# Finer steps in the attention part of a gated cross-attention and expert block: layer norms by pairs of blocks, a bias product in two parts, another order of TensorE's work

## The chip, the core and the metric

One core of a Trainium2 chip runs the whole program in one launch. The metric is the device time of one execution in microseconds (us). Five engines work side by side, each through its own queue in order: TensorE (PE in the rows; its loads of weights are PEld), VectorE (DVE), ScalarE (ACT), GpSimd (POOL) and SyncE (SP). They meet at semaphores only: an instruction waits until a counter has reached a value, and everything behind it in its queue waits too.

## What is computed

Inputs are `x` and a context, both 8 blocks x 128 rows x 128 columns, float32. Cut to what matters:

```
x = x + tanh(g_xattn) * attention(q = layernorm(x), k = v = context)    # Wq, Wk, Wv, Wo, biases; softmax per block
x = x + tanh(g_ffn)   * ffn(layernorm(x))
ffn(y)    = shared(y) + routed(y)
shared(y) = (silu(y @ w1) * (y @ w2)) @ w3       # hidden width 512
routed(y) = sum over 16 experts of gate * swiglu(y), hidden width 128;
            the gates are the sigmoid scores of the 2 best experts of each row
layernorm = (x - mean) / sqrt(var + 1e-5)        # no learned weights
```

## The kernel before

A row of a block lies in a partition; a block of 128x128 is the unit. The 8 blocks are two halves of 4 (`HALF`), and a half is two pairs of blocks. There is no scheduler: each engine's queue is written out by hand, in the order in which it stands in the code, with the waits between engines written by hand too. So a step that stands ahead of another in a queue is done first, even if it must wait and the other could go.

**The attention part, one half after the other.** DVE takes the statistics of the blocks (`block_stats`, `moments`: L549, L555, L557), POOL raises variance plus epsilon to the power -0.5 for a half at a time (`inverse_deviation`, L376, tile `rstd`), and the blocks are normalised into `xn`. PE turns them (transposes against `ident`), ACT copies them to `xnT`. Wq and Wk are fused into `qk_w`, Wv and Wo into `vo_w`. PE then makes g = `qk_w` x `xnT` for pair p (`query_key`, L831), ACT copies it to `gT` (`copy_g`), PE makes the scores (`attention_scores`, L836), DVE the row maxima, ACT the exponentials (`probs`), PE turns them (`turn_probs`), a copy gives `probsT`, and PE multiplies them with `vo` (`attend`, L848). `vo` is context x `vo_w` (`value_output`, L827) plus `vo_bias`. That bias row is the sum of two products in one bank (`fused_bias`): bv against Wo turned (L876), and a column of ones against the row bo (L877). DVE adds the attention to `x` (`add_attention`, L616) and gets `x2`.

**The second layer norm.** The statistics of `x2` follow (`second_stats`); POOL gives `rstd` again; of each half DVE normalises the first two blocks (L568) and ACT the last two (L453, with `shift` = -mean x rstd from DVE). PE turns the pairs (`turn_x2n_pair`, L858), DVE and ACT copy one pair each to `x2nT`.

**The products.** Work goes by chunks k. `share_up(k)` (L927, L928) multiplies 512 columns of `x2nT` by two blocks of weights, ACT takes the silu (L484), DVE multiplies to `hid` (L648), `share_down(k)` (L944) multiplies that by the third block. Chunks 0 to 3 are the shared part of the first half, 4 to 7 of the second half, 8 to 12 two often-used experts; then small tiles of the other experts follow. The router's logits need `x2nT` of both halves and stand on PE between `share_down(2)` and `share_down(3)`. The second half's attention, from its second transposes of `probs` on, is worked in between the first chunks: `share_up(0)`, `turn_probs(2)`, `share_up(1)`, `turn_probs(3)`, `attend(2)`, `attend(3)`, `share_down(0)`, `share_up(2)`, `share_down(1)`, `share_up(3)`, then the transposes of the second half's `x2n`. `keep_warm` (L807) issues products whose result nobody reads.

## Time and profile before

| | us |
|---|---|
| median of 3 runs (lowest to highest) | 74.22 (73.93 to 74.92) |
| the profiled execution | 73.88 |
| its span, first to last instruction | 72.2 |
| PE busy in the span | 60.9 (84%) |
| DVE, ACT, POOL busy | 38.8, 26.0, 11.7 |

The profiled execution's own time is 1.68 us more than its span: what lies around the instructions. Times in rows are from the span's start. Each matrix product in float32 shows as two matmul records with one load of weights each. Matmuls are pipelined: a record lasts longer than the distance to the next one, so a series is costed by the distance between starts.

### The profile page before, as it was taken

What the parts mean: (1) busy time and instruction counts of PE and PEld (TensorE: products, weight loads), DVE (VectorE), ACT (ScalarE), POOL (GpSimd) and SP (SyncE); (2) the same over time, 40 slices, a digit from 0 to 9 for tenths busy, and PEclk for the clock granted to TensorE, in tenths of its full rate; (3) what the DMA queues carried; (4) which work ended last, traced back from release to release, by engine and by line L of the source; (5) the groups of instructions that cost most, each with busy time, mean ns of one, the idle gap of its engine ahead of it and who ended that gap; (6) DMA issues with size and microseconds to landing.
All of it is one profiled execution on the core that took longest, in us unless ns stands there. A gap on an engine that the chain in (4) does not pass through costs nothing.

```text
span 72.2 us, 1153 instructions
## 1 busy us (share of the span) xinstructions
PE 60.9 (84%) x341; PEld 42.9 (60%) x342; DVE 38.8 (54%) x159; ACT 26.0 (36%) x71; POOL 11.7 (16%) x26
## 2 busy tenths in 40 slices
PE   1997998596979995999999999999999999996200
PEld 0335877574744564576984577475676998884100
DVE  2074824688332259833569795864730398765300
ACT  0334858043738930044411323031156823332000
POOL 4005099804100000140000000000005260000000
PEclk9999999999999999999999999999999999999985
DMA  0898470000000000000000000610698300000560
GB/s 0 229 321 203 119 313 24 0 0 0 0 0 9 0 0 5 0 0 0 0 0 0 0 0 5 189 37 0 198 283 250 145 5 0 0 0 5 148 157 13
DMA packets 5084, 4.80 MB, mean 66 GB/s; under 512 B 336, under 2 KB 4816, under 8 KB 5072
## 3 DMA queue, kind: packets, MB, share of 16 engines
q1 hardware_dynamic: 3984, 3.93, 17.8%
q10 hardware_dynamic: 1088, 0.74, 3.6%
q14 instruction: 9, 0.07, 0.3%
q8 instruction: 3, 0.05, 0.3%
HBM read 4.15 MB, written 0.52 MB: 65 GB/s over the span
## 4 chain that ended last, share of the span: by engine, by line
PE 72%; DVE 9%; DMA 4%; issue 3%; ACT 3%; POOL 1%; DVEq 0%; POOLq 0%
PE bank L944 15%; PE bank L927 15%; PE bank L928 14%; DMA x_sb<-in_x_dram 4%; PE bank L831 3%; PE bank L827 3%; PE bank L1013 3%; PE bank L822 2%; PE bank L965 2%; PE bank L836 2%; PE bank L848 2%; PE bank L1005 2%; PE bank L1004 2%; DVE hid L648 2%; PE bank L807 1%
## 5 line engine op out<-in xcount | busy, mean ns | idle before, releaser
L648 DVE TENSOR_TENSOR hid<-silu_t,bank 128x512 f32<-128x512 f32 (+1 forms) x13 | 8.4, 645 | 9.8 <-ACT silu_t L484 8.5
L484 ACT ACTIVATE silu_t<-bank 128x512 f32<-128x512 f32 (+1 forms) x13 | 7.3, 563 | 15.3 <-PE bank L928 15.3
L944 PEld LDWEIGHTS bank<-shared_sb,hid 128*128 128x128 f32 x64 | 8.1, 191 | 3.7 <-issue 1.9
L944 PE MATMUL bank<-shared_sb,hid 128*128 128x128 f32 x64 | 8.7, 280 | 0.9 <-DVE hid L648 0.9
L927 PE MATMUL bank<-x2nT,shared_sb 128*128 128x512 f32 x16 | 8.3, 603 | 0.6 <-ACT x2nT L475 0.6
L928 PE MATMUL bank<-x2nT,shared_sb 128*128 128x512 f32 x16 | 8.2, 592 | 0.0
L376 POOL TENSOR_TENSOR rstd<-var_eps,neg_half 128x4 f32<-128x4 f32 x4 | 4.1, 1018 | 21.3 <-DVE var_eps L557 21.3
L807 PE MATMUL bank<-warm_rows 128*128 128x512 bf16 x14 | 5.3, 530 | 1.6 <-DVE warm_rows L578 1.5
L410 POOL TENSOR_TENSOR acc<-acc,gated 128x512 f32<-128x512 f32 x2 | 2.5, 1270 | 24.9 <-ACT gated L494 24.9
L928 PEld LDWEIGHTS bank<-x2nT,shared_sb 128*128 128x128 f32 x16 | 3.0, 190 | 3.8 <-issue 3.8
L944 PEld LDWEIGHTS bank<-dense_w,hid 128*128 128x128 f32 x32 | 4.1, 191 | 1.9 <-issue 1.0
L944 PE MATMUL bank<-dense_w,hid 128*128 128x128 f32 x32 | 4.5, 278 | 0.7 <-DVE hid L648 0.7
L927 PE MATMUL bank<-x2nT,dense_w 128*128 128x512 f32 (+1 forms) x10 | 4.4, 518 | 0.0
L928 PE MATMUL bank<-x2nT,dense_w 128*128 128x512 f32 (+1 forms) x10 | 4.3, 507 | 0.0
L807 PEld LDWEIGHTS bank<-warm_rows 128*128 128x128 bf16 x15 | 1.8, 128 | 4.0 <-issue 2.2
L848 PE MATMUL bank<-vo,probsT 128*128 128x128 f32 x16 | 2.7, 292 | 1.2 <-DVE probsT L602 1.1
L453 ACT ACTIVATE x2n<-x,shift,rstd 128x128 f32<-128x128 f32 x4 | 1.7, 484 | 5.4 <-DVE shift L563 5.4
L1013 PE MATMUL bank<-tile_w,tile_hid 128*128 128x128 f32 x16 | 3.2, 294 | 0.2 <-DVE tile_hid L672 0.2
L501 ACT ACTIVATE tile_silu<-bank 128x128 f32<-128x128 f32 x8 | 2.1, 282 | 3.4 <-PE bank L1005 3.4
L927 PEld LDWEIGHTS bank<-x2nT,shared_sb 128*128 128x128 f32 x16 | 2.5, 193 | 1.2 <-issue 1.2
L848 PEld LDWEIGHTS bank<-vo,probsT 128*128 128x128 f32 x16 | 2.1, 190 | 1.8 <-DVE vo L592 1.3
L684 DVE SCALAR_TENSOR_TENSOR acc<-bank,tile_gates,acc 128x128 f32 x8 | 2.8, 348 | 0.7 <-issue 0.3
(135 smaller groups left out, 103.1 us busy)
## 6 DMA issues: line engine op xcount, KB each, us to landing
tile_w<-in_routed_w_dram SPq DMA_DIRECT2D x8, 192.0 KB, 3.6
shared_sb<-in_shared_w_dram SPq DMA_DIRECT2D x1, 768.0 KB, 4.5
dense_w<-in_routed_w_dram SPq DMA_DIRECT2D x2, 192.0 KB, 2.5
params<-in_attn_params_dram ACTq DMA_DIRECT2D x1, 265.0 KB, 4.1
ctx_sb<-in_ctx_dram SPq DMA_DIRECT2D x1, 256.0 KB, 4.0
x_sb<-in_x_dram SPq DMA_DIRECT2D x1, 256.0 KB, 5.6
ctx_sb<-in_ctx_dram ACTq DMA_DIRECT2D x1, 256.0 KB, 5.8
out_dram<-acc SPq DMA_DIRECT2D x1, 256.0 KB, 2.6
```

Of the source, the lines that this page charges most:

```text
L376: pool.tensor_tensor(rstd[:, n, halves(h)], var_eps[:, n, halves(h)], neg_half[:, :], ALU.pow)\
L410: pool.tensor_tensor(acc[:, h * 512:(h + 1) * 512], acc[:, h * 512:(h + 1) * 512], gated[:, i % 2, :], ALU.add)\
L484: nc.scalar.activation(silu_t[:, k % 2, columns(k)], bank[up_bank(k)][:, columns(k)], ACT.Silu).then_inc(silu_ready, 1)
L648: nc.vector.tensor_tensor(hid[:, k % HID_RING, columns(k)], silu_t[:, k % 2, columns(k)], bank[up_bank(k) + 1][:, columns(k)], ALU.mult)\
L684: nc.vector.scalar_tensor_tensor(acc[:, bass.ds(to, D)], tile_down_bank(t), tile_gates[:, t:t + 1], acc[:, bass.ds(to, D)], ALU.mult, ALU. ...
L807: nc.tensor.matmul(bank[spare][:, :], warm_rows[:, 0:P], warm_rows[:, :], start=True, stop=True)
L827: last = nc.tensor.matmul(bank[7 - h][:, b * P:(b + 1) * P], ctxT[:, HALF * h + b, :], vo_w[:, :], start=True, stop=True)
L848: last = nc.tensor.matmul(bank[S_BANK[p]][:, (b % 2) * P:(b % 2 + 1) * P], probsT[:, b, :], vo[:, b, :], start=True, stop=True)
L927: nc.tensor.matmul(bank[up_bank(k)][:, columns(k)], w1, xt, start=True, stop=True)
L928: nc.tensor.matmul(bank[up_bank(k) + 1][:, columns(k)], w2, xt, start=True, stop=True).then_inc(up_done, 1)
L944: last = nc.tensor.matmul(down_bank(k, b)[:, b * P:(b + 1) * P], hid[:, k % HID_RING, b * P:(b + 1) * P], down_weights(k), start=first and ...
L1013: nc.tensor.matmul(tile_down_bank(t), tile_hid[:, t % 3, :], tile_w[:, t % W_RING, 2 * P:3 * P], start=True, stop=True)\
```

## The change

Six things are edited, all in the attention part and the second layer norm up to the first products.

1. The first half's first layer norm goes by pairs: `x_loaded` has one semaphore for each of the three loads of x, and `moments`, `inverse_deviation` and the normalising work on PARTS: blocks 0 and 1, blocks 2 and 3, blocks 4 to 7. POOL computes three powers instead of two, here and in the second layer norm.
2. The bias product is in two parts: the product with bv stays behind `query_key(0)`, the product with ones moves between the scores of pair 0 and pair 1.
3. `turn_probs(1)` moves ahead of `attend(0)`; the turning of `xn`'s second half ahead of `value_output(1)`.
4. The first half's second layer norm goes by pairs too. DVE normalises blocks 0, 1 and 2, ACT only block 3. `values(1)` moves behind the row maxima of pairs 2 and 3. Pair 0 is turned into bank 3 instead of bank 6, between `query_key(3)` and the scores of pairs 2 and 3. Both calls of `keep_warm` there are gone.
5. Chunk 0's products go by pairs of blocks, 256 columns each.
6. On DVE `share(0)` stands ahead of `add_attention(2)`, and `second_stats(2)` ahead of `add_attention(3)`.

```diff
+        PARTS = (slice(0, 2), slice(2, 4), slice(4, 8))
...
-            def inverse_deviation(n, h):
-                pool.wait_ge(var_ready, 2 * n + h + 1)
-                pool.tensor_tensor(rstd[:, n, halves(h)], var_eps[:, n, halves(h)], neg_half[:, :], ALU.pow)\
+            def inverse_deviation(n, m):
+                pool.wait_ge(var_ready, 3 * n + m + 1)
+                part = PARTS[m]
+                pool.tensor_tensor(rstd[:, n, part], var_eps[:, n, part], neg_half[:, 0:part.stop - part.start], ALU.pow)\
                     .then_inc(rstd_ready, 1)
...
-            normalise(0)
+            normalise((3,), 1)
             act.wait_ge(x2n_pair_turned, 2)
...
-            dve.wait_ge(x_loaded[0], 16 * 2)
-            block_stats(0, x_sb, range(HALF))
-            moments(0, 0)
-            dve.wait_ge(rstd_ready, 1)
-            normalise(0, x_sb, xn, range(HALF), xn_by_dve)
-            dve.wait_ge(x_loaded[1], 16)
+            for m in range(2):
+                dve.wait_ge(x_loaded[m], 16)
+                block_stats(0, x_sb, range(2 * m, 2 * m + 2))
+                moments(0, m)
+            for m in range(2):
+                dve.wait_ge(rstd_ready, m + 1)
+                normalise(0, x_sb, xn, range(2 * m, 2 * m + 2), xn_by_dve)
+            dve.wait_ge(x_loaded[2], 16)
...
-            add_attention(0)
-            second_stats(0)
-            add_attention(1)
-            second_stats(1)
-            moments(1, 0)
-            values(1)
-            shifts(0)
+            for p in range(2):
+                add_attention(p)
+                second_stats(p)
+                moments(1, p)
+            dve.wait_ge(rstd_ready, 4)
             normalise(1, x2, x2n, (0, 1), x2n_by_dve)
             dve.wait_ge(x2n_pair_turned, 1)
-            nc.vector.tensor_copy(x2nT[:, 0:256], bank[6][:, 0:256]).then_inc(x2nT_ready[0], 1)
+            nc.vector.tensor_copy(x2nT[:, 0:256], bank[3][:, 0:256]).then_inc(x2nT_ready[0], 1)
+            shifts(1)
+            normalise(1, x2, x2n, (2,), x2n_by_dve)
             row_maxima(2)
             row_maxima(3)
+            values(1)
...
+            def first_share_up():
+                w1, w2 = up_weights(0)
+                for p in range(2):
+                    pe.wait_ge(x2nT_ready[p], 1)
+                    c = slice(256 * p, 256 * p + 256)
+                    nc.tensor.matmul(bank[up_bank(0)][:, c], w1, x2nT[:, c], start=True, stop=True)
+                    last = nc.tensor.matmul(bank[up_bank(0) + 1][:, c], w2, x2nT[:, c], start=True, stop=True)
+                last.then_inc(up_done, 1)
...
             pe.wait_ge(x2_ready, HALF)
-            share_up(0)
+            first_share_up()
             turn_probs(2)
+            pe.wait_ge(vo_ready[1], 1)
             share_up(1)
```

PE's queue around the bias product, before. Bank 6 takes the bias product, banks 0 and 1 take g, banks 2 and 3 the scores:

```order
L831 MATMUL bank0<-xnT,qk_w 128x256 [waits xnT_ready0,fused_ready]
L876 MATMUL bank6<-woT,params 128x128 [waits vo_w_ready,rows_loaded,consts_ready]
L877 MATMUL bank6<-rows,ones_row 128x128
L831 MATMUL bank1<-xnT,qk_w 128x256 [waits xnT_ready1]
L836 MATMUL bank2<-ctxT,gT 128x128 [waits g_ready0,ctxT_ready0]
L836 MATMUL bank2<-ctxT,gT 128x128
L836 MATMUL bank3<-ctxT,gT 128x128 [waits g_ready1]
L836 MATMUL bank3<-ctxT,gT 128x128
```

And of the changed kernel, where the lines are numbered otherwise (L838 is `query_key`, L843 the scores, L890 and L897 the bias product's parts):

```order
L838 MATMUL bank0<-xnT,qk_w 128x256 [waits xnT_ready0,fused_ready]
L890 MATMUL bank6<-woT,params 128x128 [waits vo_w_ready]
L838 MATMUL bank1<-xnT,qk_w 128x256 [waits xnT_ready1]
L843 MATMUL bank2<-ctxT,gT 128x128 [waits g_ready0,ctxT_ready0]
L843 MATMUL bank2<-ctxT,gT 128x128
L897 MATMUL bank6<-rows,ones_row 128x128 [waits rows_loaded,consts_ready]
L843 MATMUL bank3<-ctxT,gT 128x128 [waits g_ready1]
L843 MATMUL bank3<-ctxT,gT 128x128
```

The product with ones has moved from ahead of `query_key(1)` to between the two pairs of scores.

PE's queue from `query_key(2)` to the first product, before (L858 turns `x2n`, L836 are scores, L807 the products nobody reads):

```order
L831 MATMUL bank5<-xnT,qk_w 128x256 [waits xnT_ready2]
L831 MATMUL bank4<-xnT,qk_w 128x256
L807 MATMUL bank7<-warm_rows 128x512 x2
L836 MATMUL bank5<-ctxT,gT 128x128 [waits g_ready2]
L836 MATMUL bank5<-ctxT,gT 128x128
L836 MATMUL bank4<-ctxT,gT 128x128 [waits g_ready3]
L836 MATMUL bank4<-ctxT,gT 128x128
L807 MATMUL bank7<-warm_rows 128x512 x3
L858 MATMUL bank6<-ident,x2n 128x128 [waits x2n_by_dve,vo_ready1]
L858 MATMUL bank6<-ident,x2n 128x128
L858 MATMUL bank7<-ident,x2n 128x128 [waits x2n_by_act]
L858 MATMUL bank7<-ident,x2n 128x128
L927 MATMUL bank2<-x2nT,shared_sb 128x512 [waits x2nT_ready0,x2_ready,shared_loaded]
```

And of the changed kernel (L867 turns `x2n`, L940 and L941 are the first chunk's products by pairs):

```order
L838 MATMUL bank5<-xnT,qk_w 128x256 [waits xnT_ready2]
L838 MATMUL bank4<-xnT,qk_w 128x256
L867 MATMUL bank3<-ident,x2n 128x128 [waits x2_ready,x2n_by_dve]
L867 MATMUL bank3<-ident,x2n 128x128
L843 MATMUL bank5<-ctxT,gT 128x128 [waits g_ready2]
L843 MATMUL bank5<-ctxT,gT 128x128
L843 MATMUL bank4<-ctxT,gT 128x128 [waits g_ready3]
L843 MATMUL bank4<-ctxT,gT 128x128
L867 MATMUL bank7<-ident,x2n 128x128 [waits x2n_by_act,x2n_by_dve]
L867 MATMUL bank7<-ident,x2n 128x128
L940 MATMUL bank2<-x2nT,shared_sb 128x256 [waits x2nT_ready0,x2_ready,shared_loaded]
L941 MATMUL bank3<-x2nT,shared_sb 128x256
```

The turning of pair 0 now stands ahead of the scores, with a wait for DVE, and the five products on `warm_rows` are gone.

DVE's queue from the second half's scale to the second product, before (L648 is `hid`, L616 adds the attention):

```order
L609 TENSOR_SCALAR att_scale<-inv_sum,tanh_g 128x4 [waits tanh_ready,inv_ready]
L616 SCALAR_TENSOR_TENSOR x2<-bank5,att_scale,x_sb 128x128 [waits pv_done,att_scale_ready]
L616 SCALAR_TENSOR_TENSOR x2<-bank5,att_scale,x_sb 128x128
L648 TENSOR_TENSOR hid<-silu_t,bank3 128x512 [waits silu_ready]
L616 SCALAR_TENSOR_TENSOR x2<-bank4,att_scale,x_sb 128x128 [waits pv_done,att_scale_ready]
L616 SCALAR_TENSOR_TENSOR x2<-bank4,att_scale,x_sb 128x128
L549 BN_STATS stats<-x2 128x6 [waits x2_ready]
L549 BN_STATS stats<-x2 128x6
L549 BN_STATS stats<-x2 128x6 [waits x2_ready]
L549 BN_STATS stats<-x2 128x6
L648 TENSOR_TENSOR hid<-silu_t,bank7 128x512 [waits silu_ready]
L555 BN_AGGR mean_var<-stats 128x2 [waits stats_ready] x4
```

And of the changed kernel (L655 is `hid`, L622 adds the attention):

```order
L615 TENSOR_SCALAR att_scale<-inv_sum,tanh_g 128x4 [waits tanh_ready,inv_ready]
L655 TENSOR_TENSOR hid<-silu_t,bank3 128x512 [waits silu_ready]
L622 SCALAR_TENSOR_TENSOR x2<-bank5,att_scale,x_sb 128x128 [waits pv_done,att_scale_ready]
L622 SCALAR_TENSOR_TENSOR x2<-bank5,att_scale,x_sb 128x128
L553 BN_STATS stats<-x2 128x6 [waits x2_ready]
L553 BN_STATS stats<-x2 128x6
L622 SCALAR_TENSOR_TENSOR x2<-bank4,att_scale,x_sb 128x128 [waits pv_done,att_scale_ready]
L622 SCALAR_TENSOR_TENSOR x2<-bank4,att_scale,x_sb 128x128
L553 BN_STATS stats<-x2 128x6 [waits x2_ready]
L553 BN_STATS stats<-x2 128x6
L655 TENSOR_TENSOR hid<-silu_t,bank7 128x512 [waits silu_ready]
L559 BN_AGGR mean_var<-stats 128x2 [waits stats_ready] x4
```

`hid` of chunk 0 has moved ahead of both additions, and both additions with their statistics now stand between it and `hid` of chunk 1.

## Rows read from the trace of the kernel before

**Rows 1.** The page: the clock granted to TensorE, in 40 slices of the span (tenths)

```profile
PEclk9999999999999999999999999999999999999985
```

**Rows 2.** Busy time of each engine in three stretches

```profile
core 0: us, PE busy (x) PEld busy (x) DVE busy (x) ACT busy (x) POOL busy (x), PEclk, DMA share, GB/s
12.20:15.60 3.40, 2.31 (x17) 1.83 (x16) 2.46 (x9) 1.30 (x4) 2.01 (x10) 1.00 0.00 0
15.60:19.00 3.40, 2.67 (x17) 2.10 (x19) 2.78 (x13) 1.15 (x3) 1.04 (x1) 1.00 0.00 0
28.00:59.00 31.00, 30.98 (x174) 21.71 (x175) 18.61 (x82) 9.78 (x24) 3.55 (x3) 1.00 0.21 64
```

**Rows 3.** The chain that ended last, around the bias product (start us, us, what)

```profile
8.91 0.41 PE bank L877 x2
...
10.52 0.71 PE bank L836 x4
```

**Rows 4.** Instructions in order of time, from 3.8 to 10 us

```profile
3.81 0.87 DVE L549 BATCH_NORM_STATS2 stats<-x_sb 128x6 f32<-128x128 f32 x4 [2.34 <-DMA x_sb<-in_x_dram]
...
5.00 0.17 DVE L557 TENSOR_SCALAR var_eps<-mean_var 128x4 f32<-128x4 f32 x1
5.32 1.02 POOL L376 TENSOR_TENSOR rstd<-var_eps,neg_half 128x4 f32<-128x4 f32 x1 [3.60 <-DVE var_eps L557]
...
7.74 0.38 PE L869 MATMUL bank<-ident,xn 128*128 128x128 f32 x2
...
8.42 0.38 ACT L432 COPY xnT<-bank 128x256 f32<-128x256 f32 x1
...
9.26 0.70 PE L831 MATMUL bank<-xnT,qk_w 128*128 128x256 f32 x2
...
9.79 1.44 PE L836 MATMUL bank<-ctxT,gT 128*128 128x128 f32 x8
...
10.02 3.12 POOL L384 TENSOR_SCALAR xn<-x_sb,mean_var,rstd 128x128 f32<-128x128 f32 x4
```

**Rows 5.** The same from 14 to 22 us

```profile
14.21 0.61 DVE L616 SCALAR_TENSOR_TENSOR x<-bank,att_scale,x_sb 128x128 f32<-128x128 f32 x2 [0.59 <-PE bank L848]
...
14.86 0.49 DVE L549 BATCH_NORM_STATS2 stats<-x 128x6 f32<-128x128 f32 x2
...
15.59 0.61 DVE L616 SCALAR_TENSOR_TENSOR x<-bank,att_scale,x_sb 128x128 f32<-128x128 f32 x2 [0.25 <-PE bank L848]
...
17.29 1.04 POOL L376 TENSOR_TENSOR rstd<-var_eps,neg_half 128x4 f32<-128x4 f32 x1 [3.00 <-DVE var_eps L557]
...
18.44 0.60 DVE L568 TENSOR_SCALAR x2n<-x,mean_var,rstd 128x128 f32<-128x128 f32 x2
...
19.24 0.86 ACT L453 ACTIVATE x2n<-x,shift,rstd 128x128 f32<-128x128 f32 x2
...
20.63 0.60 PE L858 MATMUL bank<-ident,x2n 128*128 128x128 f32 x4
...
21.27 0.37 ACT L475 COPY x2nT<-bank 128x256 f32<-128x256 f32 x1 [1.17 <-PE bank L858]
...
21.79 1.10 PE L927 MATMUL bank<-x2nT,shared_sb 128*128 128x512 f32 x2 [0.55 <-ACT x2nT L475]
```

**Rows 6.** The chain again: transposes of `probs`, `share_down(1)`, `share_down(2)`

```profile
25.68 0.23 PE bank L842 x2
...
30.90 0.89 PE bank L944 x8
...
33.95 1.01 PE bank L944 x8
```

**Rows 7.** Instructions in order of time, from 27 to 34 us

```profile
27.29 0.68 DVE L648 TENSOR_TENSOR hid<-silu_t,bank 128x512 f32<-128x512 f32 x1
...
29.18 0.67 DVE L648 TENSOR_TENSOR hid<-silu_t,bank 128x512 f32<-128x512 f32 x1
...
33.06 0.69 DVE L648 TENSOR_TENSOR hid<-silu_t,bank 128x512 f32<-128x512 f32 x1 [0.91 <-ACT silu_t L484]
```

More of the change, by code:

```diff
@@ L175, in flamingo_block @@
         ctx_loaded = [sem(f"ctx_loaded{i}") for i in range(2)]
-        x_loaded = [sem(f"x_loaded{i}") for i in range(2)]
+        x_loaded = [sem(f"x_loaded{i}") for i in range(3)]
         shared_loaded = sem("shared_loaded")
@@ L220, in flamingo_block @@
         x2n_turned = sem("x2n_turned")
-        x2nT_ready = [sem(f"x2nT_ready{i}") for i in range(2)]
+        x2nT_ready = [sem(f"x2nT_ready{i}") for i in range(3)]
         x2n_pair_turned = sem("x2n_pair_turned")
@@ L399, in _ @@
                                base=0, pattern=[[1, P]], channel_multiplier=-1).then_inc(route_consts_ready, 1)
-            inverse_deviation(1, 0)
-            inverse_deviation(1, 1)
+            for m in range(3):
+                inverse_deviation(1, m)
             for k in range(FIRST_DENSE, FIRST_DENSE + BY_POOL):
@@ L890, in _ @@
             attention_scores(0)
+            pe.wait_ge(consts_ready, 2)
+            pe.wait_ge(rows_loaded, 16)
+            nc.tensor.matmul(bank[6][:, P:2 * P], ones_row[:, :], bo_row, start=False, stop=True).then_inc(fused_done, 1)
             attention_scores(1)
```

84 lines of the change are left out of this document (39 added, 45 removed).

## The prediction

> **What bounds the kernel now.** Read the busy time by stretches first. From 28 to 59 us PE is busy 30.98 of 31.00 us, and in the two stretches between 12.2 and 19 us only 2.31 and 2.67 of 3.40 [rows 2]. So the program is two things: up to 28 us a ladder of short steps that hand over between engines, and then a block of TensorE work with no holes. None of the change's edits takes useful work out of that block. What it can gain is an earlier start of the block, and what it can lose is a hole in it. The question is therefore when `hid` of chunk 0 ends (27.29 + 0.68 = 27.97 [rows 7]), since `share_down(0)` and everything behind it follows, and whether the DVE work that the change pushes behind it comes late for something. Then read the chain of waits and the order of time through the ladder, and ask at each rung: does this instruction start when its data are there, or only when its own queue gets to it?
>
> **Part a: up to the scores of pair 1.** In the chain the product with ones takes 0.41 us [rows 3], the one with bv ahead of it has two records of 0.11, and both stand between `query_key(0)` and `query_key(1)`. `query_key(1)` starts at 9.26, though its `xnT` was copied by 8.42 + 0.38 = 8.80 [rows 4]. So 0.46 us there is waiting in PE's own queue, not for data.
> The layer norm by pairs, step by step. Four blocks of statistics take 0.87 us and the epsilon step starts 1.19 us after the first of them (3.81 to 5.00). With two blocks fewer I take 0.70, so it starts at 4.51 and ends at 4.68; POOL starts about 0.10 later, at 4.78. The power of 4 columns takes 1.02 [rows 4]. The trace has none of 2 columns. Its cost lies between 0.51 (all of it goes by columns) and 1.02 (none of it does). The only row is that of 4 columns, so I take 1.02, the end that this row states. Then pair 0's power ends at 5.80, where the whole half's ended at 6.34: pair 0 is 0.54 early. Pair 1's power queues behind it on POOL, ends at 6.82, and pair 1 is normalised by 7.46, as before (about 7.48). So the pairs help pair 0 alone, and pair 1 gains only what PE's queue gave away: its turning starts at about 7.53 instead of 7.74 [rows 4]. The ACT copies in front are done earlier too, thanks to pair 0, so that `xnT` of pair 1 is ready at 7.53 + 0.48 + 0.41 = 8.42, and `query_key(1)` starts at 8.52, 0.74 early.
> From there to the scores of pair 1 it was 10.52 - 9.26 = 1.26 [rows 3, 4], so they could start at 9.78. But the product with ones now stands in front of them: the scores of pair 0 start 0.53 behind `query_key(1)`, at 9.05; eight records of scores are 0.11 apart, so four take 0.43, and with 0.10 of transition and 0.41 the product with ones is through at 9.99; I take 9.95. The gain is 10.52 - 9.95 = 0.57. With the cheap power it would be `query_key(1)` at 8.31 and 9.78 at the scores, 0.74. The low end is 0.2, if the product with ones holds up the scores longer than its 0.41.
>
> **Part b: to the attention's addition.** From the scores of pair 1 to `x2` of pair 0 it was 14.21 - 10.52 = 3.69 [rows 3, 5], through `value_output(0)`, the addition of the bias on DVE, the copy of `probsT` and `attend(0)`. All of it stands in the same order. `turn_probs(1)` now waits for the last exponential ahead of `attend(0)`, but PE sat idle there for the copy, and two transposes are 0.23 us [rows 6]. Cost 0. It brings `attend(1)` forward, which is the cover that part c needs: `x2` of pair 1 came 1.38 us behind pair 0 [rows 5], and will again, though four small steps are put between them. The addition starts at 13.64.
>
> **Part c: from the first addition to the first product.** Before, 21.79 - 14.21 = 7.58 us [rows 5]. Count what the data alone need in the new order, from the start of the first addition: addition and wait 0.65 (14.21 to 14.86); statistics of two blocks, aggregates, epsilon start 0.67; next instruction 0.08: 1.40. The same again for pair 1: 2.80. DVE normalises two blocks, 0.60: 3.40. Turning and handing over 0.47: 3.87. DVE copies, 0.43: 4.30. The shift and its handing over, in part under the copy: 4.42. ACT normalises one block, 0.48 (half of 0.86, a little more): 4.90. PE turns pair 1, 0.05 + 0.25 later the first product starts: 5.20 to 5.25. POOL's power for pair 1 starts at 2.97 and ends by 4.05 even at 1.04 us, hidden under the turning and the copy. The gain is 7.58 - 5.25 = 2.33 us.
> Where did the time lie before? `x2n` was whole at 19.24 + 0.86 = 20.10, but PE turned it at 20.63, behind the scores and the products on `warm_rows`; and the power started at 17.29 because it waited for all four blocks [rows 5]. ACT's part started 0.80 behind DVE's because ACT was copying g.
> Can PE keep up? `attend(0)` starts 0.80 ahead of the addition, at 12.84. Behind it, at 0.11 a record: the second half of its own four records and a hand-over 0.43, four transposes 0.43, `attend(1)` 0.43, four transposes 0.43, eight records of values 0.86 and `query_key(2)` and (3) 0.86 give 16.4 with a wait or two. Pair 0's `x2n` is there at 13.64 + 3.45 = 17.1. So PE waits 0.7 us in `turn_x2n_pair(0)`, with the scores of pairs 2 and 3 queued behind it; DVE's row maxima for these wait in turn, but stand behind `x2n` of block 2 anyway. POOL's second half of `xn` is done at 13.14 [rows 4], ahead of its turning at about 14.2. The second half's `values(1)`, 0.69 us of DVE, is out of this stretch, which is part of the 2.33. Bounds from the neighbours: 1.8 (every hand-over 0.05 longer, ten of them) to 2.6.
>
> **Part d: from the first product to `hid` of chunk 0.** Before, 27.97 - 21.79 = 6.18. Chunk 0 by 256 columns issues the same columns; I allow 0.04. The chain turns the `probs` of pair 3 from 25.68 [rows 6], and behind their copy and the scale stood one addition, then `hid`. An addition of two blocks is 0.61 long [rows 5], 0.54 of it before the next instruction starts. This addition now comes behind `hid`. ACT's silu of chunk 0 waits for the second half's exponentials and a load of tables. They start 0.9 us behind the turning of pair 1 and are through about 1.3 us before `hid`, as I count it. Gain 0.50.
>
> **Part e: what is late behind `hid` of chunk 0.** Before, `hid` of chunk 1 started 29.18 - 27.97 = 1.21 us behind it. Now two additions and two pairs of statistics lie between: 0.65 + 0.43 + 0.65 + 0.41, less 0.09 of overlap, 2.05. `share_down(1)` was due 30.90 - 27.97 = 2.93 behind [rows 6], and `hid` of chunk 1 ends at 2.05 + 0.68 = 2.73: covered, by 0.2. But the second half's statistics, power and normalising follow it, and ACT normalises blocks 6 and 7 ahead of the silu of chunk 2. From the start of `hid` of chunk 1 to the end of that of chunk 2 it was 33.75 - 29.18 = 4.57 [rows 7], so now it ends at 6.62, and `share_down(2)`, which stood at 33.95 - 27.97 = 5.98 [rows 6], waits until 6.65. A hole of 0.67 us in the block, and the logits and the router move with it. Bounds: 0.3 to 0.9.
>
> **Sum.** 0.57 + 2.33 + 0.50 - 0.67 = 2.73 us. 73.88 - 2.73 = 71.15 against the profiled execution, which was 0.34 below the median of 74.22; with half of that, **71.3**. The ends of the parts, not all at once, give 70.4 to 72.1.
>
> **Rivals.** (1) TensorE's clock. The granted clock is full until the last slices, after PE has gone quiet [rows 1]. The change takes out the five products on `warm_rows` and puts in a wait of 0.7 us at about 16.5, then one of 0.4. Fell the clock there from 2.4 to 1.2 GHz until `share_down(0)`, the 6.1 us of records up to it (transposes 0.88, scores 0.86, products 3.5, `attend` 0.86) would take twice as long, less 1.1 of waits that this fills: 5.0 more, 76.1 us. It turns into a loss against before once more than 2.7 us of records fall at the lower level. Against it: from 12.2 to 15.6 PE was busy 2.31 of 3.40, and the clock stayed at 1.00 [rows 2]. The new stretch packs the same work closer.
> The Trainium skill speaks for this rival: TensorE: Matmul & The Clock Gate, Part 4 (PE-mode transpose), says that transposes don't count as activity for the full clock as products do. The stretch of 12.2 to 15.6 holds six transposes among 17 records and kept 1.00, which bears out at most that such a mixture is enough here; no row shows one without `warm_rows` ahead of the products.
> (2) PE comes late to `turn_x2n_pair(0)`. The margin is 0.7 us. Were the turned `xn` and its copy, now ahead of `value_output(1)`, or the wait for `ctxT` 2 us late, 1.3 would be lost: 72.6.
> (3) The pairs and the split product give nothing, since the second power queues on POOL and the ones product stands in front of the scores: part a is 0, 71.9. That is the form in which the change would not do what it says.
> (4) The hole grows: `hid` of chunk 1 misses its 0.2 of cover too and the router's steps on DVE fall behind PE, 1.5 instead of 0.67: 72.1, with part c at its low end 72.7.
>
> **How the numbers follow.** Forecast 0.70; (1) 0.08, of which 0.05 in full; (2) 0.06; (3) 0.09; (4) 0.07. A measurement of this kernel can tell some 2% from no change, so faster means below 72.74 and slower above 75.70. Faster holds the forecast, (3) and most of (2) and (4), 0.84; slower the full form of (1), 0.05; the rest is 0.11. For 8 in 10 the range goes from 70.4 to 72.9.
>
> **What would show it.** `query_key(1)` starts near 8.5 and the scores of pair 1 near 9.95, right behind the product with ones. Two powers of about 1 us stand back to back on POOL near 4.8 and 5.8. The first product starts near 18.9, 5.2 us behind the first addition. PE idles ahead of the turning of pair 0. `hid` of chunk 0 ends near 24.5. One new wait stands in the block, of 0.6 to 0.7 us at `share_down(2)`; behind it PE is full as before. I am wrong if the granted clock dips between 16 and 25 us, if PE's idle time at the first turning is gone (then PE, not DVE, sets part c), or if the block has other holes.

## The result

The changed kernel takes 71.48 us (70.98 to 71.82, 4 runs) against 74.08 us before (4 runs): ratio 0.9665, 95% interval 0.9622 to 0.9708. Measured a second time beside other kernels it gave 0.966 (0.959 to 0.9731). It is faster, by 2.6 us; 71.3 was forecast. Executions more than 1.5% above a kernel's fastest are left out of the ratios here and below, but are in the medians.

The profiled execution took 71.56 us, its span is 69.7. The page of the changed kernel, busy time and the two rows over 40 slices:

```profile
PE 60.0 (86%) x341; PEld 42.9 (62%) x341; DVE 39.7 (57%) x162; ACT 25.5 (37%) x70; POOL 12.5 (18%) x28
...
PE   1999998796899989979999999999999999995100
...
PEclk9999999999999999999999999999999999999985
```

Beside [rows 1] the granted clock reads the same: full until the last slices. The stretches, laid where the same work now is:

```profile
core 0: us, PE busy (x) PEld busy (x) DVE busy (x) ACT busy (x) POOL busy (x), PEclk, DMA share, GB/s
12.20:15.60 3.40, 2.99 (x24) 2.75 (x25) 2.75 (x13) 1.47 (x3) 1.81 (x10) 1.00 0.00 0
15.60:19.00 3.40, 2.60 (x18) 1.95 (x16) 2.80 (x14) 1.47 (x4) 1.33 (x2) 1.00 0.00 0
...
24.70:56.50 31.80, 31.21 (x174) 21.49 (x175) 19.33 (x85) 9.78 (x24) 3.54 (x3) 1.00 0.20 63
```

From 12.2 to 15.6 PE is busy 2.99 of 3.40, where it was 2.31 [rows 2]. And the block behind `share_down(0)`, which had no hole, has one. PE is busy 31.21 of 31.80; 0.11 of the rest lies ahead of `share_down(0)`, which starts at 24.81, and 0.48 is the wait shown below.

The changed kernel's instructions in order of time, from 4 to 12 us. Its lines are L878 for the turning of `xn`, L838 for `query_key`, L843 for the scores, L821 to L825 for the fusing of the weights, L890 and L897 for the two bias products:

```profile
4.43 0.17 DVE L561 TENSOR_SCALAR var_eps<-mean_var 128x2 f32<-128x2 f32 x1
...
4.75 1.43 POOL L380 TENSOR_TENSOR rstd<-var_eps,neg_half 128x2 f32<-128x2 f32 x2 [3.04 <-DVE var_eps L561]
...
5.50 1.32 DVE L572 TENSOR_SCALAR xn<-x_sb,mean_var,rstd 128x128 f32<-128x128 f32 x4
5.77 0.35 PE L821 MATMUL bank<-ident,params 128*128 128x128 f32 x1
...
6.48 0.49 PE L825 MATMUL bank<-woT,params 128*128 128x128 f32 x2
...
6.81 0.38 PE L878 MATMUL bank<-ident,xn 128*128 128x128 f32 x2
...
7.74 0.67 PE L838 MATMUL bank<-xnT,qk_w 128*128 128x256 f32 x2
...
8.57 0.70 PE L838 MATMUL bank<-xnT,qk_w 128*128 128x256 f32 x2
...
9.13 0.68 PE L843 MATMUL bank<-ctxT,gT 128*128 128x128 f32 x4
...
9.75 0.48 PE L897 MATMUL bank<-rows,ones_row 1*128 1x128 f32 x2
...
10.16 0.52 PEld L843 LDWEIGHTS bank<-ctxT,gT 128*128 128x128 f32 x4
```

`xn` of pair 0 is done at about 6.1, but PE turns it at 6.81: it is still at the weights. Before, PE had been through with those by 6.19 + 0.49 and waited for `xn` until 7.03. `query_key(1)` starts at 8.57 (9.26 in [rows 4]), and the scores of pair 1 at 10.16, right behind the product with ones. POOL's two powers take 1.43 together.

The second layer norm and the first products of the changed kernel (L622 adds the attention, L867 turns `x2n`, L940 is the first product):

```profile
16.77 0.59 DVE L572 TENSOR_SCALAR x2n<-x,mean_var,rstd 128x128 f32<-128x128 f32 x2
16.94 0.72 POOL L380 TENSOR_TENSOR rstd<-var_eps,neg_half 128x2 f32<-128x2 f32 x1 [0.73 <-DVE var_eps L561]
...
17.42 0.44 PE L867 MATMUL bank<-ident,x2n 128*128 128x128 f32 x2 [0.55 <-DVE x2n L572]
...
17.70 1.06 PE L843 MATMUL bank<-ctxT,gT 128*128 128x128 f32 x8
...
18.42 0.49 ACT L457 ACTIVATE x2n<-x,shift,rstd 128x128 f32<-128x128 f32 x1 [1.04 <-DVE shift L567]
...
19.06 0.41 PE L867 MATMUL bank<-ident,x2n 128*128 128x128 f32 x2 [0.31 <-ACT x2n L457]
...
19.30 0.60 PE L940 MATMUL bank<-x2nT,shared_sb 128*128 128x256 f32 x2
...
19.51 0.37 ACT L479 COPY x2nT<-bank 128x256 f32<-128x256 f32 x1 [0.59 <-PE bank L867]
...
24.07 0.68 DVE L655 TENSOR_TENSOR hid<-silu_t,bank 128x512 f32<-128x512 f32 x1
...
26.74 0.67 DVE L655 TENSOR_TENSOR hid<-silu_t,bank 128x512 f32<-128x512 f32 x1
...
29.22 0.88 ACT L457 ACTIVATE x2n<-x,shift,rstd 128x128 f32<-128x128 f32 x2 [5.46 <-DVE shift L567]
...
30.01 0.57 ACT L488 ACTIVATE silu_t<-bank 128x512 f32<-128x512 f32 x1
...
30.25 0.63 PE L829 MATMUL bank<-ident,x2n 128*128 128x128 f32 x4
...
30.61 0.69 DVE L655 TENSOR_TENSOR hid<-silu_t,bank 128x512 f32<-128x512 f32 x1 [0.91 <-ACT silu_t L488]
...
31.36 1.16 PE L958 MATMUL bank<-shared_sb,hid 128*128 128x128 f32 x8 [0.48 <-DVE hid L655]
```

In [rows 5] the turning started at 20.63 and the first product at 21.79. Now pair 0 is turned at 17.42 as soon as DVE has it (PE waited 0.55 us for it), and the first product starts at 19.30. At `share_down(2)` stands the new wait: 0.48 us for `hid` of chunk 2, whose silu started at 30.01 only, behind ACT's 0.88 us of normalising. The same place before:

```profile
33.34 0.60 PE L822 MATMUL bank<-ident,x2n 128*128 128x128 f32 x4
...
33.80 1.16 PE L944 MATMUL bank<-shared_sb,hid 128*128 128x128 f32 x8
```

From the transposes to `share_down(2)` it was 0.46 us from start to start, now it is 1.11: the wait is worth 0.65.

Both executions cut into stages, by starts of instructions read from the two traces (us). The spans are printed to 0.1 only, so the last row and the sum are good to some 0.05:

| stage | before | changed | gain |
|---|---|---|---|
| start to `query_key(0)` | 8.02 | 7.74 | 0.28 |
| to the first addition of attention | 6.19 | 6.11 | 0.08 |
| to the first product | 7.58 | 5.45 | 2.13 |
| to the start of `hid` of chunk 0 | 5.50 | 4.77 | 0.73 |
| to `share_down(2)` | 6.51 | 7.29 | -0.78 |
| to the end of the last addition | 34.05 | 34.05 | 0.00 |
| to the end of the span | 4.35 | 4.29 | 0.06 |
| sum | 72.20 | 69.70 | 2.50 |

From `share_down(2)` to the last addition the two kernels take the same 34.05 us. All of the change's effect lies ahead of it.

### The profile page after: what moved, and what is told of

The parts are those of the page before. It is cut to its first block, busy times and chain, and to the rows that moved or that the text cites. A ratio compares the mean times of both kernels' runs of the same rounds, so it can differ in the third digit from the quotient of the medians.

```text
span 69.7 us, 1158 instructions
## 1 busy us (share of the span) xinstructions
PE 60.0 (86%) x341; PEld 42.9 (62%) x341; DVE 39.7 (57%) x162; ACT 25.5 (37%) x70; POOL 12.5 (18%) x28
## 4 chain that ended last, share of the span: by engine, by line
PE 66%; DVE 17%; issue 5%; ACT 3%; POOL 1%; DVEq 0%
PE bank L958 13%; PE bank L931 12%; PE bank L932 11%; PE bank L814 6%; DVE hid L655 4%; DVE x L622 3%; PE bank L1028 3%; DVE stats L553 3%; PE bank L980 2%; PE bank L1019 2%; PE bank L1020 2%; ACT silu_t L488 2%; PE bank L838 2%; PE bank L843 2%; POOL rstd L380 1%
## 5 line engine op out<-in xcount | busy, mean ns | idle before, releaser
L655 DVE TENSOR_TENSOR hid<-silu_t,bank 128x512 f32<-128x512 f32 (+1 forms) x13 | 8.4, 644 | 9.3 <-ACT silu_t L488 8.1
L488 ACT ACTIVATE silu_t<-bank 128x512 f32<-128x512 f32 (+1 forms) x13 | 7.3, 563 | 14.8 <-PE bank L932 14.8
L958 PEld LDWEIGHTS bank<-shared_sb,hid 128*128 128x128 f32 x64 | 8.0, 191 | 3.8 <-DVE hid L655 2.3
L958 PE MATMUL bank<-shared_sb,hid 128*128 128x128 f32 x64 | 8.8, 280 | 0.7 <-DVE hid L655 0.7
L380 POOL TENSOR_TENSOR rstd<-var_eps,neg_half 128x2 f32<-128x2 f32 (+1 forms) x6 | 4.9, 811 | 18.0 <-DVE var_eps L561 18.0
L931 PE MATMUL bank<-x2nT,shared_sb 128*128 128x512 f32 x14 | 7.2, 599 | 0.0
L932 PE MATMUL bank<-x2nT,shared_sb 128*128 128x512 f32 x14 | 7.1, 592 | 0.0
L814 PE MATMUL bank<-warm_rows 128*128 128x512 bf16 x10 | 4.5, 632 | 1.5 <-DVE warm_rows L582 1.5
L958 PEld LDWEIGHTS bank<-dense_w,hid 128*128 128x128 f32 x32 | 4.1, 192 | 1.9 <-issue 1.0
L958 PE MATMUL bank<-dense_w,hid 128*128 128x128 f32 x32 | 4.5, 278 | 0.7 <-DVE hid L655 0.7
L932 PEld LDWEIGHTS bank<-x2nT,shared_sb 128*128 128x128 f32 x14 | 2.7, 190 | 3.3 <-issue 3.3
L457 ACT ACTIVATE x2n<-x,shift,rstd 128x128 f32<-128x128 f32 x3 | 1.4, 487 | 6.5 <-DVE shift L567 6.5
L553 DVE BATCH_NORM_STATS2 stats<-x_sb 128x6 f32<-128x128 f32 x8 | 1.8, 281 | 2.6 <-DMA x_sb<-in_x_dram 2.6
L388 POOL TENSOR_SCALAR xn<-x_sb,mean_var,rstd 128x128 f32<-128x128 f32 x4 | 3.1, 794 | 0.1
L1019 PE MATMUL bank<-x2nT,tile_w 128*128 x16 | 3.1, 275 | 0.0
L1020 PE MATMUL bank<-x2nT,tile_w 128*128 x16 | 3.1, 275 | 0.0
```

Source lines behind the costliest of these rows:

```text
L380: pool.tensor_tensor(rstd[:, n, part], var_eps[:, n, part], neg_half[:, 0:part.stop - part.start], ALU.pow)\
L388: pool.tensor_scalar(xn[:, b, :], x_sb[:, b, :], mean_var[:, 0, b, 0:1], rstd[:, 0, b:b + 1], ALU.subtract, ALU.mult)\
L488: nc.scalar.activation(silu_t[:, k % 2, columns(k)], bank[up_bank(k)][:, columns(k)], ACT.Silu).then_inc(silu_ready, 1)
L553: nc.vector.bn_stats(stats[:, n, k, :], src[:, k, :]).then_inc(stats_ready, 1)
L655: nc.vector.tensor_tensor(hid[:, k % HID_RING, columns(k)], silu_t[:, k % 2, columns(k)], bank[up_bank(k) + 1][:, columns(k)], ALU.mult)\
L814: nc.tensor.matmul(bank[spare][:, :], warm_rows[:, 0:P], warm_rows[:, :], start=True, stop=True)
```

## The experiments

Each kernel is the changed one with one edit, so each is to be read against 71.5; only the last in the table has three edits and is to be read against the early `hid`. The medians of small edits carry some 0.2 to 0.3 us of scatter. In the traces it is the two ends that vary: the opening (below), and the stretch behind the last addition, 4.0 to 4.5 us in twelve of the profiled executions and 5.5 in two. The stages between are sharper: between kernels that don't touch a stage they agree within 0.02 us. So the verdicts rest on the stages, in this table of differences of starts in each kernel's one profiled execution, with the medians beside them.

| kernel | median us | ratio to before | start to `query_key(0)` | to first addition | to first product | to `hid` 0 | to `share_down(2)` |
|---|---|---|---|---|---|---|---|
| before | 74.08 | 1 | 8.02 | 6.19 | 7.58 | 5.50 | 6.51 |
| changed | 71.48 | 0.9665 | 7.74 | 6.11 | 5.45 | 4.77 | 7.29 |
| changed, again | 71.49 | 0.966 | 8.36 | 6.11 | 5.45 | 4.77 | 7.28 |
| early `hid` of chunk 2 | 70.69 | 0.9549 | 7.54 | 6.10 | 5.46 | 4.77 | 6.63 |
| second norm whole | 72.68 | 0.974 | 7.99 | 6.11 | 6.35 | 6.45 (clock fell) | 7.28 |
| 9 opening products | 71.62 | 0.965 | 7.75 | 6.10 | 5.46 | 4.76 | 7.29 |
| `values(1)` back | 72.18 | 0.9728 | 8.30 | 6.11 | 6.07 | 4.76 | 7.29 |
| turning behind scores | 72.03 | 0.9741 | 7.78 | 6.11 | 6.02 | 4.84 | 7.28 |
| edit 6 undone | 71.62 | 0.9704 | 7.70 | 6.10 | 5.46 | 5.42 | 6.51 |
| `warm_rows` back | 71.70 | 0.9684 | 8.20 | 6.11 | 5.61 | 4.76 | 7.29 |
| first norm whole | 71.84 | 0.9724 | 8.30 | 6.10 | 5.45 | 4.77 | 7.29 |
| bias product whole | 71.67 | 0.9669 | 7.93 | 6.19 | 5.46 | 4.76 | 7.29 |
| `turn_probs(1)` back | 71.47 | 0.9658 | 8.21 | 6.10 | 5.46 | 4.77 | 7.28 |
| early `hid`, short opening | 72.73 | - | 7.92 | 6.10 | 5.46 | 4.76 | 6.64 |

**The hole at `share_down(2)`: pull `hid` of chunk 2 forward.**

```diff
             share(1)                                    # ACT
-            normalise((6, 7), 2)
             share(2)
+            normalise((6, 7), 2)
...
             moments(1, 2)                               # DVE
+            share(2)
             shifts(2)
             normalise(1, x2, x2n, (HALF, HALF + 1), x2n_by_dve)
-            share(2)
```

> The changed kernel with chunk 2 pulled forward: DVE does hid of chunk 2 right behind moments(1, 2), while POOL computes the power, and ACT takes the silu of chunk 2 ahead of normalising blocks 6 and 7. If the new wait at share_down(2) comes from ACT's normalising and DVE's norm work standing ahead of chunk 2 (part e), PE's wait there goes, share_down(2) starts at 30.8 to 30.9 instead of 31.36, and the time falls by 0.45 us, to about 71.0. If the hole is only the first of a series (the router or hid of chunk 3 is late as well), the wait moves behind and the time stays within 0.1 of 71.5.

Measured: 70.69 us, ratio 0.9549 (0.9495 to 0.9603). The last stage is 6.63 instead of 7.29. Its instructions in order of time (L488 is the silu, L655 `hid`, L958 `share_down`, L457 ACT's normalising):

```profile
27.52 0.60 ACT L488 ACTIVATE silu_t<-bank 128x512 f32<-128x512 f32 x1 [3.96 <-PE bank L932]
27.53 0.17 DVE L561 TENSOR_SCALAR var_eps<-mean_var 128x4 f32<-128x4 f32 x1
27.78 1.01 POOL L380 TENSOR_TENSOR rstd<-var_eps,neg_half 128x4 f32<-128x4 f32 x1 [10.32 <-DVE var_eps L561]
28.15 0.69 DVE L655 TENSOR_TENSOR hid<-silu_t,bank 128x512 f32<-128x512 f32 x1 [0.45 <-ACT silu_t L488]
...
28.82 0.16 DVE L567 SCALAR_TENSOR_TENSOR shift<-mean_var,rstd 128x4 f32<-128x4 f32 x1
28.90 0.60 DVE L572 TENSOR_SCALAR x2n<-x,mean_var,rstd 128x128 f32<-128x128 f32 x2
29.02 0.88 ACT L457 ACTIVATE x2n<-x,shift,rstd 128x128 f32<-128x128 f32 x2 [0.90 <-DVE shift L567]
...
30.50 1.06 PE L958 MATMUL bank<-shared_sb,hid 128*128 128x128 f32 x8
```

DVE does `hid` of chunk 2 at 28.15, while POOL computes the power from 27.78, and `share_down(2)` shows no wait. So the hole was order in two queues, not a lack of time, and nothing moved in behind it. The gain of 0.66 in the stage is the 0.65 that the wait was worth. This version beats both kernels.

**The second layer norm as a whole again.**

```diff
-            for m in range(3):
-                inverse_deviation(1, m)
...
+            pool.tensor_tensor(rstd[:, 1, halves(0)], var_eps[:, 1, halves(0)], neg_half[:, :], ALU.pow).then_inc(rstd_ready, 1)
...
                 second_stats(p)
-                moments(1, p)
+            for k in range(HALF):
...
+                nc.vector.bn_aggr(mean_var[:, 1, k, :], stats[:, 1, k, :]).then_inc(moments_ready, 1)
```

> The changed kernel with the first half's second layer norm as before: statistics and one power of 4 columns for all four blocks, everything else as changed. If the pairs are worth something because POOL's power of pair 0 hides under pair 1's addition, then x2n of blocks 0 and 1 comes 1.2 us later, PE turns it near 18.7 instead of 17.42, and the first product starts 0.75 us later: 72.2 us. If the gain of part c came from the order of PE's queue and from moving values(1) alone, it stays at 71.5.

Measured: 72.68 us, ratio 0.974 (0.9671 to 0.9809), which of 74.08 is 72.2 us; the ratio rests on three executions of five, and its interval is wide, so the stage decides. The stage to the first product is 6.35, 0.90 more. PE turns pair 0 at 18.56 and had waited 1.44 us for it. Taken away from the whole change, the pairs cost 0.9 of its 2.13. (In this profiled execution the granted clock fell for a while, so its stage to `hid` 0 is long; see the last section.)

**`values(1)` back ahead of the normalising.**

```diff
                 moments(1, p)
+            values(1)
             dve.wait_ge(rstd_ready, 4)
...
             row_maxima(3)
-            values(1)
```

> The changed kernel with values(1) (0.69 us on DVE) put back ahead of normalising x2n. If DVE's queue sets this rung, as part c counts, the turning of pair 0 and the first product come 0.65 us later, 72.1 us. If PE's queue sets it (rival 2), nothing changes.

Measured: 72.18 us, ratio 0.9728 (0.9671 to 0.9784), the stage 0.62 longer, close to the 0.69 of the instruction. DVE's queue sets this rung.

**The turning of pair 0 behind the scores again.**

```diff
             query_key(3)
-            turn_x2n_pair(0)
             attention_scores(2)
             attention_scores(3)
+            turn_x2n_pair(0)
             turn_x2n_pair(1)
```

> The changed kernel with turn_x2n_pair(0) behind the scores of pairs 2 and 3 again, without the products on warm_rows. The scores could start at 17.0 when g of pair 2 is there; pair 0 would be turned at about 17.95 instead of 17.42, and the copies and the shift behind it on DVE follow. By part c the first product comes 0.4 us later: 71.9 us. If the wait in PE's queue ahead of the scores costs as much as it brings, 71.5.

Measured: 72.03 us, ratio 0.9741 (0.9695 to 0.9787), the stage 0.57 longer. PE's wait of 0.55 us ahead of the scores is well spent.

**The products on `warm_rows` back.**

```diff
             query_key(3)
+            keep_warm(2, 7)
             turn_x2n_pair(0)
...
             attention_scores(3)
+            keep_warm(3, 7)
             turn_x2n_pair(1)
```

> The changed kernel with both series of products on warm_rows put back, 2 ahead of the turning of pair 0 and 3 behind the scores. The granted clock is 1.00 in the changed kernel from 12 to 22 us, so nothing is won; the first two lie in PE's wait, the last three (0.65 us) in a wait of 0.3 to 0.5: 0.15 us later, 71.6. If they held the clock in some executions (rival 1), this kernel would be faster than 71.5 or vary less.

Measured: 71.70 us, ratio 0.9684 (0.9624 to 0.9744), the stage 0.16 longer as expected. Of its four executions one took 73.53 with a mean granted clock of 0.955: the products didn't keep that away.

**Edit 6 undone.**

```diff
-            share(0)
             add_attention(2)
-            second_stats(2)
+            share(0)
             add_attention(3)
+            second_stats(2)
             second_stats(3)
```

> The changed kernel with edit 6 undone: add_attention(2) ahead of hid of chunk 0, add_attention(3) ahead of second_stats(2). By parts d and e this gives back 0.50 to 0.55 at hid of chunk 0 and wins back the wait of 0.5 to 0.6 at share_down(2): the time stays within 0.15 of 71.5. If the hole has another cause, the time rises by 0.5.

Measured: 71.62 us, ratio 0.9704 (0.9676 to 0.9733). `hid` of chunk 0 starts 0.65 later, and the last stage is 6.51 as before, without the hole. Over both stages it is 11.93 against 12.06: edit 6 alone bought nothing and cost 0.13. With the early `hid` of chunk 2 beside it, it is 11.40. The early `hid` without edit 6 was not run; with no wait at `share_down(2)` there, it has nothing to take away.

**The opening, one product on `warm_rows` less.**

```diff
-            keep_warm(10, 7)
+            keep_warm(9, 7)
```

> The changed kernel with 9 instead of 10 opening products on warm_rows. In the changed kernel's trace the transpose of Wo starts at 5.77, behind the last of them, and xn of pair 0 is ready before PE gets to it at 6.81. If PE's opening series is what swallowed 0.2 of part a's 0.57, the transpose starts at 5.4, xn is turned at 6.4 to 6.5 and the time falls by 0.2 to 0.35 us. Rival: the granted clock comes later for it and the first float32 products run longer; then 71.5 or more.

Measured: 71.62 us, ratio 0.965 (0.9595 to 0.9706): no difference. Neither forecast holds as it stood. In the profiled execution PE was free earlier, and then waited for the load of the parameters, as the row of this kernel in order of time says:

```profile
5.83 0.30 PE L821 MATMUL bank<-ident,params 128*128 128x128 f32 x1 [0.45 <-DMA params<-in_attn_params_dram]
```

That load landed 4.4 us behind its issue here, and 4.0 in the changed kernel's first execution, where PE came to the parameters at 5.77 without a wait. So with nine products the load can be what sets the start, and how often it is, one trace doesn't show.

**The opening with both, the load moved and one product less, on top of the early `hid`.**

```diff
-            act.dma_start(x_sb[:, twos(1), :], x_dram[:, twos(1), :]).then_inc(x_loaded[1], 16)
             act.dma_start(params[:, :], attn_params).then_inc(params_loaded, 16)
+            act.dma_start(x_sb[:, twos(1), :], x_dram[:, twos(1), :]).then_inc(x_loaded[1], 16)
...
-            keep_warm(10, 7)
+            keep_warm(9, 7)
```

> The early hid of chunk 2, and the opening shortened: 9 opening products on warm_rows instead of 10, and the parameters' load ahead of that of x blocks 2 and 3 in ACT's queue. With 9 products alone PE then waited for the parameters until 5.83. If the opening is bound by both, the transpose of Wo starts at 5.4, xn of pair 0 is turned at 6.4 instead of 6.8, and the time is 0.3 us below the kernel with the early hid alone, 70.4 us. If x of pair 1 arrives too late for its normalising, or the full clock later, it stays at 70.7 or above.

Measured: 72.73 us (71.41 to 73.1), a miss. Four of its six executions took 72.54 to 73.1, so no ratio was formed; the other two, 71.41 and 72.12, are about 1 us above the 70.37 to 71.24 of the early `hid` alone. The loads of parameters and x (KB, us from issue to landing), and rows in order of time:

```profile
params<-in_attn_params_dram ACTq DMA_DIRECT2D x1, 265.0 KB, 3.3
...
x_sb<-in_x_dram SPq DMA_DIRECT2D x1, 128.0 KB, 3.6
x_sb<-in_x_dram ACTq DMA_DIRECT2D x1, 128.0 KB, 3.6
```

```profile
4.46 0.49 DVE L553 BATCH_NORM_STATS2 stats<-x_sb 128x6 f32<-128x128 f32 x2 [2.98 <-DMA x_sb<-in_x_dram]
...
5.34 0.42 PE L821 MATMUL bank<-ident,params 128*128 128x128 f32 x1
...
6.27 0.47 PE L825 MATMUL bank<-woT,params 128*128 128x128 f32 x2
...
6.92 0.44 PE L878 MATMUL bank<-ident,xn 128*128 128x128 f32 x2 [0.18 <-DVE xn L572]
```

The transpose of Wo did start at 5.34. But both loads of x took 3.6 us instead of 2.9 and 3.1, the one in the other queue too, and the statistics started at 4.46 instead of 3.69. PE then waited for `xn` again, at 6.92. The start to `query_key(0)` is 7.92, no better than 7.54 to 8.36 with the old order. That accounts for 0.4 us against the early `hid`'s execution. The profiled span, 70.4, has 5.5 us behind its last addition where the early `hid`'s has 4.1. That part is not shown to be the edit's: the profiled execution with the turning behind the scores, whose opening is untouched, has the same 5.5, and is its kernel's slowest with 73.32 us. Why the stores land later in some executions no run shows, nor whether the new opening makes them more frequent.

**The first layer norm as a whole again.**

```diff
-            for m in range(2):
-                dve.wait_ge(x_loaded[m], 16)
-                block_stats(0, x_sb, range(2 * m, 2 * m + 2))
-                moments(0, m)
-            for m in range(2):
-                dve.wait_ge(rstd_ready, m + 1)
-                normalise(0, x_sb, xn, range(2 * m, 2 * m + 2), xn_by_dve)
...
+            block_stats(0, x_sb, range(HALF))
...
+            dve.wait_ge(rstd_ready, 2)
+            normalise(0, x_sb, xn, range(HALF), xn_by_dve)
```

> The changed kernel with the first half's first layer norm as before: one semaphore value for both loads, one power of 4 columns. By part a the pairs are worth what PE can use of them: PE is busy until 6.8 anyway, the first turning would start at 7.0, and the scores of pair 1 come 0.2 to 0.3 us later: 71.7 to 71.8. If PE's opening series swallows all of it, 71.5.

Measured: 71.84 us, ratio 0.9724 (0.9686 to 0.9762), 0.35 above the changed kernel. In its trace the product with Wo turned starts at 6.55 and `query_key(0)` at 8.30, 1.75 apart; in the changed kernel it is 7.74 - 6.48 = 1.26, and before it was 8.02 - 6.19 = 1.83. So the pairs are worth 0.5 us from the weights on, when PE is through with the weights that early and at the full clock. In three executions with the pairs in which the first float32 products still ran at the lower level (the changed kernel again, `values(1)` back, `warm_rows` back) the same distance is 1.66, 1.60 and 1.50, and `query_key(0)` starts at 8.20 to 8.36, where it is 8.30 in this kernel without the pairs. There PE is late, and the pairs bring next to nothing.

**The bias product whole again.**

```diff
             nc.tensor.matmul(bank[6][:, P:2 * P], bv_col.to_broadcast([P, P]), woT[:, :], start=True, stop=False)
...
+            nc.tensor.matmul(bank[6][:, P:2 * P], ones_row[:, :], bo_row, start=False, stop=True).then_inc(fused_done, 1)
...
             attention_scores(0)
...
-            nc.tensor.matmul(bank[6][:, P:2 * P], ones_row[:, :], bo_row, start=False, stop=True).then_inc(fused_done, 1)
             attention_scores(1)
```

> The changed kernel with both parts of the bias product in a row again, ahead of query_key(1). By part a the ones product costs 0.41 us of PE's time in either place, and what it fills at the new place is a wait for g of pair 1 of only some 0.1 to 0.2: the scores of pair 1 come 0.1 later than in the changed kernel (10.25 to 10.3 against 10.16), 71.6 us. If the split were worth its whole 0.41, 71.9.

Measured: 71.67 us, ratio 0.9669 (0.9606 to 0.9732). From `query_key(0)` to the first addition it is 6.19, as before the change, against 6.11: the split is worth 0.08 us.

**`turn_probs(1)` behind `attend(0)` again.**

```diff
-            turn_probs(1)
             pe.wait_ge(vo_ready[0], 1)
             attend(0)
+            turn_probs(1)
```

> The changed kernel with turn_probs(1) behind attend(0) again. Part b costs the move at 0: attend(1) would end about 0.7 us later, at 15.2, and add_attention(1) starts at 15.31, so it is just covered: 71.5 us, within 0.1. If it isn't covered, every step from pair 1's addition on is 0.1 to 0.4 later.

Measured: 71.47 us, ratio 0.9658 (0.9606 to 0.971), and no stage differs. The additions of pair 0 and pair 1 start at 14.31 and 15.77, 1.46 apart as in the changed kernel. The move is worth nothing.

**The changed kernel again.**

> The changed kernel itself, unedited, beside the next kernels on their chip: 71.5 us, ratio 0.965 to 0.97. It shows how far one kernel's median moves between series, against which edits worth 0.1 to 0.4 us are to be read.

Measured: 71.49 us (70.95 to 73.52, 7 runs), ratio 0.966 (0.959 to 0.9731). The stages up to `share_down(2)` are the same but for the opening, 8.36 us against 7.74.

**What was not undone by itself.** Edit 5, DVE's normalising of block 2, and the earlier turning of `xn`'s second half have no run of their own. For edit 5 the rows say what it must be worth: ACT copies pair 1 of `x2nT` from 19.51 to 19.88, and the products of pair 0 start at 19.30. A product over all 512 columns could not have started before 19.88, as the one before waited 0.55 us for that copy [rows 5]. So some 0.6 us of the 2.13 needs edit 5 too; this is an estimate.

## Why the prediction was right, step by step

**Part a, forecast 0.57, measured 0.36.** In the forecast's own rungs `query_key(1)` started at 8.57 for 8.52, and the scores of pair 1 at 10.16 for 9.95. So 0.05 of the missing 0.21 lies ahead of `query_key(1)` and 0.16 behind it. There the scores of pair 0 came 0.56 behind it for 0.53, the product with ones 0.62 behind them (9.13 to 9.75) for 0.53, and the sum of 9.99 had been taken as 9.95.

That `query_key(1)` was met within 0.05 is luck, since two errors cancel in it. The power was priced too dear: of 2 columns it takes 0.72 us, between the two ends given, not the 1.02 that was taken, and with the cheap end the forecast itself had 8.31; in the early `hid`'s execution, whose weights came 0.20 earlier, it is 8.37. And the term took for granted that PE would be at hand. Its fusing of the weights, finished by 6.68 before, ended by 6.97 in this execution, 0.29 later, since the first records of PE ran at the lower clock for longer (below); no edit reaches there. Before, that lateness would have been hidden under the wait for `xn` (0.35 us); the pairs took the wait away, and with it the cover. This is the question that part a left out: what is late next. From the weights to `query_key(0)` the change gained 0.57 (1.83 to 1.26), the split of the bias product 0.08, and the opening took 0.29 back.

**Part b, forecast 0, measured 0.** The way from the scores of pair 1 to the first addition is 13.85 - 10.16 = 3.69, as before, and the undone move confirms that it costs and brings nothing.

**Part c, forecast 2.33, measured 2.13.** DVE's queue sets it, as forecast, and PE's wait in front of the turning was 0.55 for the forecast 0.7. The missing 0.2 lies in small steps: from the start of the statistics of two blocks to the epsilon step it took 0.74, not 0.67, twice (14.49 to 15.23, 15.95 to 16.69); turning pair 0 and handing it to the copy took 0.54 for 0.47 (17.36 to 17.90); and ACT's block reached PE 0.15 behind its end for 0.05 (18.91 to 19.06). Undone one at a time, the pairs are worth 0.90, `values(1)` 0.62, the turning ahead of the scores 0.57. These overlap with each other, with the removed products (0.16) and with edit 5, so the single undos are not shares of one sum. Rival 2 (PE late to the turning) is refuted by `values(1)` back: there PE waits 1.2 us at the turning, and nearly all of DVE's delay comes through (0.62 of 0.69).

**Parts d and e, forecast 0.50 and -0.67, measured 0.73 and -0.78.** Both terms were somewhat small, and the sum was close: -0.17 forecast, -0.05 measured. For d, undoing edit 6 costs 0.65 of the 0.73 in that stage, where the forecast had 0.54 for the addition less 0.04 for the products by pairs; the other 0.08 no run explains. For e, the forecast had `hid` of chunk 2 end 6.62 behind that of chunk 0, and it was 6.55 (24.75 to 31.30). The size of the hole was off by a reading: `share_down(2)` was taken to start at 33.95, from the chain [rows 6], but a row of the chain begins where the piece ahead of it ends, and in order of time the instruction starts at 33.80. With that the forecast's own sum is 0.82 for the measured 0.78. `share_down(1)` was read so too, at 30.90 for 30.73, and its cover of 0.2 was really 0.03; that `hid` of chunk 1 still came in time (ended at 27.41, PE started at 27.52 without a wait) was closer than the forecast knew. The place and the cause of the hole were right, as the early `hid` shows by taking away 0.66 us of it. Rival 4 (the hole grows) did not come: from `share_down(2)` to the last addition it is 34.05 us in both kernels.

**Rival 1, the clock,** did not set the time: the granted clock is 1.00 over the stretches of 12.2 to 19 us and over the block, and with the products on `warm_rows` back nothing is faster. But it was not empty. Single executions of the changed kernel do fall to the lower level, at another place than the rival named (below). The kernel with the second norm whole, whose wait at the turning is 1.44 us, fell in the rival's own place, from 20.5 us on. And the rival's price was too high: a fall lasted 3.4 us and cost 1.7, not 5.0. **Rival 3** is refuted by both undos of part a.

The sum of 2.73 against 2.50 in the profiled executions is part a's 0.2 and part c's 0.2, less 0.12 in d and e and 0.06 behind the last addition, which is within the rounding of the spans.

## What to carry to other kernels

Where engines hand over in a ladder, cost a reordering by counting the shortest chain of hand-overs from one rung to the next, and then ask of each other queue whether it is there in time; the wait that the edit takes away may have been covering a lateness of exactly that queue. Work pushed behind the critical instruction comes back as a wait some chunks later: look there for a step that can be done while another engine is computing, before giving the first gain back. Take the start of an instruction from the order of time: a row of the chain starts where the piece ahead of it ends. And judge edits worth a few tenths of a microsecond by the stage in the trace, not by the median, when the opening alone varies by more.
